# Moving pad stores, scatters, early results and sums in a fused attention and expert kernel

## The reference

```
x = x + lightning_attn(layernorm(x))   # 16 heads, chunked linear attention with decay
x = x + ffn(layernorm(x))              # 32 experts, first use
x = x + softmax_attn(layernorm(x))     # 16 heads, 4 shared key/value heads
x = x + ffn(layernorm(x))              # 32 experts, second use, the same weights

ffn(x):  probs = softmax(x @ gate_weight.T);  top_vals, top_idx = top_k(probs, 8)
         keep the first experts until their renormalised sum reaches 0.8, renormalise
         out  = sum over kept experts e of  ce[e] * (silu(g_e) * u_e) @ down_e.T
                with  g_e, u_e = split(x @ gate_up_e.T)      # 96 values each
```

## Time and profile before

| what | value |
|---|---|
| runs | 1075.89, 1076.09, 1078.5 us, median 1076.09 |
| profiled execution | 1081.71 us, span 1079.9 us |
| PE / DVE / ACT / POOL busy | 883.9 / 581.2 / 554.6 / 627.0 us of the span |
| lightning | 0 to 268 us |
| experts "f" | 269 to 509 us |
| attention | 510 to 804.5 us |
| experts "g" | 805 to 1079.9 us |

### The profile page before, as it was taken

One profiled execution on the slowest core, in us unless ns is written; L12 is line 12 of the kernel. 1 busy time (PEld: TensorE's weight loads), 2 busy tenths in 40 slices (PEclk: granted clock), 3 DMA queues, 4 the chain that ended last, 5 costly groups with the idle time before them and its releaser, 6 DMA issues. The chain is left out here.

```text
span 1079.9 us, 20627 instructions
## 1 busy us (share of the span) xinstructions
PE 883.9 (82%) x5504; PEld 670.5 (62%) x5504; DVE 581.2 (54%) x2104; ACT 554.6 (51%) x1116; POOL 627.0 (58%) x600
## 2 busy tenths in 40 slices
PE   5999899884789799998378997987758989999940
PEld 3566666553778699997243443543328879999930
DVE  4566676866572122326776488765635422222665
ACT  6333356651345365655268776775514544556520
POOL 2465537775777777775730010374754777777771
PEclk9999989986799999999679998989887999999985
DMA  9600002261768876783431011135336788777776
GB/s 338 254 1 1 1 31 87 74 242 68 244 216 304 281 241 215 221 263 122 159 137 35 35 35 41 44 123 217 128 112 205 257 293 277 235 215 251 269 252 205
DMA packets 93231, 181.64 MB, mean 168 GB/s; under 512 B 18985, under 2 KB 73788, under 8 KB 92736
## 3 DMA queue, kind: packets, MB, share of 16 engines
q1 hardware_dynamic: 68544, 114.19, 33.1%
q0 software_dynamic: 24576, 66.13, 16.7%
HBM read 96.34 MB, written 92.27 MB: 175 GB/s over the span
## 5 line engine op out<-in xcount | busy, mean ns | idle before, releaser
L1317 POOL DMA_INDIRECT result_rows<-ys,result_slots x288 | 290.8, 1010 | 87.9 <-issue 80.6
L1002 POOL DMA_INDIRECT expert_rows<-route_rows,index x224 | 223.5, 998 | 76.8 <-issue 65.1
L1968 ACT ACTIVATE b_probs<-ps 128x1024 f32<-128x1024 f32 x128 | 127.8, 1031 | 39.5 <-PE ps L1817 39.0
L1469 PE MATMUL ps<-w_gu,g_xts 128*128 x576 | 109.0, 333 | 2.3 <-issue 1.4
L1469 PE MATMUL ps<-w_gu,f_xts 128*128 x576 | 108.5, 332 | 2.6 <-ACT f_xts L1512 1.8
L1469 PEld LDWEIGHTS ps<-w_gu,g_xts 128*128 128x128 f32 x576 | 94.5, 195 | 3.8 <-issue 3.6
L1469 PEld LDWEIGHTS ps<-w_gu,f_xts 128*128 128x128 f32 x576 | 93.9, 194 | 4.2 <-issue 4.0
L1562 DVE SCALAR_TENSOR_TENSOR g_h<-ps,g_xs,g_gate 128x96 f32<-128x96 f32 x144 | 39.3, 313 | 87.8 <-ACT g_gate L1519 78.9
L1562 DVE SCALAR_TENSOR_TENSOR f_h<-ps,f_xs,f_gate 128x96 f32<-128x96 f32 x144 | 39.2, 313 | 86.7 <-ACT f_gate L1519 77.7
L1530 ACT COPY ys<-ps 128x512 f32<-128x512 f32 x144 | 83.5, 580 | 2.0 <-PE ps L1488 1.9
L1829 PE MATMUL ps<-b_probs,b_v_pad 128*32 128x512 f32 x512 | 75.2, 661 | 11.0 <-DVE b_v_pad L2101 5.5
(11 more groups left out here) (362 smaller groups left out, 1831.8 us busy)
## 6 DMA issues: line engine op xcount, KB each, us to landing
parts<-result_rows SPq DMA_DIRECT2D x32, 896.0 KB, 4.9
f_xs<-expert_rows SPq DMA_DIRECT2D x144, 160.0 KB
g_xs<-expert_rows SPq DMA_DIRECT2D x144, 160.0 KB, 2.7
expert_rows<-pad_rows SPq DMA_DIRECT2D x64, 160.0 KB
w_gu<-in_Wgu SPq DMA_DIRECT2D x1, 6144.0 KB, 18.4
expert_rows<-pad_rows SPq DMA_DIRECT2D x1, 5120.0 KB, 29.2
result_rows<-ys,result_slots POOLq DMA_INDIRECT x288, 3.3
f_w_d<-in_Wdown SPq DMA_DIRECT2D x1, 4096.0 KB, 15.4
```

Of the source, the lines that this page charges most:

```text
L1002: self.nc.gpsimd.indirect_dma_start(xs, bass.IndirectOffsetOnAxis(self.index[:, f, t, r:r + 1].bitcast(U32), 0), self.x_rows(f)[:, t, :], ...
L1317: self.nc.gpsimd.indirect_dma_start(self.y_dram, bass.IndirectOffsetOnAxis(self.slots[:, i, j:j + 1].bitcast(U32), 0), self.ys[:, i, j, :] ...
L1469: ins = nc.tensor.matmul(ps[:, bank_gu[u % 2], j * GU:(j + 1) * GU], xts[:, u % 2, o:o + P], w_gu[:, k, bass.ds(experts[j] * GU, GU)], sta ...
L1968: nc.scalar.activation(probs[:, u % RING, :, :], ps[:, 2 * (u % 2):2 * (u % 2) + 2, :], ACT.Exp, scale=float(HD) ** -0.5).then_inc(exp_don ...
```

## The change

1. Lightning's POOL issues four scatters of batch 2 at its end (`IN_DRAIN = 4`, two each in its last two units with such places), and "f" starts batch 2 at its fifth scatter.
2. The pads go out at u = 11, 13, ..., 25 in place of 17 to 24. `pads` is worked out in routing step 12 of batch 3, behind the index, with a semaphore of its own, `padded`, and SP waits for that instead of the list.
3. PE and ACT do the routing steps of slot 0 ahead of the turn and eviction of pair 0, instead of at the end of slot 0.
4. In "g" POOL scatters the results of pairs 0 and 1 (four transfers) ahead of batch 3's scatters; in "f" none.
5. The sums of "g" start at slot 59 instead of 62. A load stands three slots behind the slot of its sum: so "g" loads where it did (62, 64, ...), and "f", whose sums stay at 66, loads at 69, 71, 73, 75.

```
-                    scattered = 0
+                    scattered = 4                                   # use "f"
+            at = 2 * (unit - B * UNITS - 2 * QUADS)                 # lightning's scatters
+            if 0 <= at < IN_DRAIN:
+                yield B - 2, at
+                yield B - 2, at + 1
...
+            if f == B - 1:                                           # step 12, DVE
+                dve.wait_ge(self.counted, f + 1)
+                nc.vector.tensor_scalar(self.pads[:, :], self.count[:, 0, :], -1.0, None, ALU.add).then_inc(self.padded, 1)
...
-                    routing.wait_tiles(sp, LAST)
+                    sp.wait_ge(routing.padded, 1)
-                if PADS_AT <= u < PADS_AT + E // PADS:
-                    store_pads(PADS * (u - PADS_AT), PADS)
+                nth = (u - PADS_AT) // PADS_EVERY                    # 11, 2
+                if (u - PADS_AT) % PADS_EVERY == 0 and 0 <= nth < E // PADS:
+                    store_pads(PADS * nth, PADS)
...
+            for step, f in steps_at(0):                              # PE; ACT the same
+                routing.tensor(pe, step, f, bank_route, apart=True)
...
+        def early_pairs(scattered):
+            return 2 if (Routing.ALL - scattered) // 2 <= placed + 1 else 0
...
+            if u == left - 1:
+                for v in range(early):
+                    yield v
...
-            first, count = (62, NT) if last else (66, TT)
+            first, count = (59, NT) if last else (66, TT)
+        def loads_at(u, last):
+            return sums_at(u - 3, last)
```

More of the change, by code:

```diff
@@ L158, in lightning @@
     WITH_POWER = 3
+    IN_DRAIN = 4
     with ExitStack() as ctx:
@@ L967, in __init__ @@
         self.chosen_ready, self.pos_ready, self.index_ready = sem("chosen_ready"), sem("pos_ready"), sem("index_ready")
-        self.counted, self.listed = sem("counted"), sem("listed")
+        self.counted, self.listed, self.padded = sem("counted"), sem("listed"), sem("padded")
         self.scattered = [sem(f"scattered{f}") for f in range(B)]
@@ L1266, in list_tiles @@
             steps(nc.vector.tensor_tensor(self.row[:, :], self.row[:, :], self.valid[:, :], ALU.add))
-            if final:
-                steps(nc.vector.tensor_scalar(self.pads[:, :], self.count[:, 0, :], -1.0, None, ALU.add))
-            else:
+            if not final:
                 steps(nc.vector.tensor_scalar(flat(self.used), flat(self.since), -1.0, float(tiles), ALU.mult, ALU.add))
@@ L1352, in experts @@
     FLUSH = 4
-    PADS_AT = 17
+    PADS_AT = 11
     PADS = 4
+    PADS_EVERY = 2
+    assert PADS_AT + PADS_EVERY * (E // PADS - 1) < (TILES - PHASES[-1][1]) // 2
     LOADED = [COVERED[sum(t >= n for n in (2 * TT, 3 * TT, 3 * TT + TT // 2))] // 2 for t in range(NT)]
@@ L1502, in _ @@
                     down(u - 3, held.pop(u - 3))
-                for step, f in steps_at(u):
+                for step, f in steps_at(u) if u > 0 else ():
                     routing.tensor(pe, step, f, bank_route, apart=True)
@@ L1531, in keep_result @@
                                ps[:, bank_y[u % 2], :].rearrange("p (j n) -> p j n", j=2)).then_inc(y_ready, 1)
+            for step, f in steps_at(0):
+                routing.scalar(act, step, f, bank_route)
             for u in range(PAIRS + FLUSH):
@@ L2270, in scatters_at @@
                 yield B - 1, at + 1
+        def early_pairs(scattered):
+            return 2 if (Routing.ALL - scattered) // 2 <= placed + 1 else 0
         def results_at(u, scattered, last):
-            left = (Routing.ALL - scattered) // 2
+            left = max((Routing.ALL - scattered) // 2, placed)
             pairs = TILES // 2 if last else TILES // 2 - LATER
-            if u == max(left, placed) + Routing.ALL // 2:
-                for v in range(pairs):
+            early = early_pairs(scattered)
+            if u == left - 1:
+                for v in range(early):
+                    yield v
+            if u == left + Routing.ALL // 2:
+                for v in range(early, pairs):
                     yield v
         def sums_at(u, last):
-            first, count = (62, NT) if last else (66, TT)
+            first, count = (59, NT) if last else (66, TT)
             at = u - first
@@ L2313, in program @@
                         lambda u: scatters_at(u, scattered), lambda u: results_at(u, scattered, final),
-                        lambda u: sums_at(u, final), lambda u: sums_at(u, final), out_rows if final else None,
+                        lambda u: loads_at(u, final), lambda u: sums_at(u, final), out_rows if final else None,
                         weights_ready(use))
```

## The result

The changed kernel took 1072.55 us (median of 20 runs, 1069.7 to 1078.53) against 1080.47 for the kernel before in the same session (20 runs, 1074.99 to 1083.84): a ratio of 0.9929, with a 95% interval of 0.9914 to 0.9944, so 0.7% faster. The forecast was 1069.4 from a median of 1076.09, a ratio of 0.9938.

The account below looks back on a forecast made before the run. No engine is full throughout; PE's waits for tiles, POOL's scatters and the end chain of loads and sums bound it. 1081.71 - 1.6 ("f") - 5.1 ("g") = 1075.0, less 5.62 to the median: 1069.4 us; range 1062.5 to 1078.

Parts of the forecast that it names:

- nothing else there is late: the barrier comes 5.1 later: End of lightning: four more scatters ahead of POOL's drain, 1.28 us each, move the barrier 5.1 us later.
- rival A: Lightning's drain: the four scatters are free there and the barrier stays, giving 1064.3 us; chance 0.13.
- -1.6: Stage "f": it ends with POOL's drain, 1.6 us earlier, though PE's chain alone would give -4.2.
- The stall it began with: "f", pairs 21 to 27: PE loses 12.1 us waiting for tiles while SP issues pads.
- What was to be left of it, 2 us: "f": with pads spread, about 2 us of PE's 12.1 us wait for tiles remain.
- Its last scatter stays at 502.4 and its drain at 507.5: POOL in "f": it loses nothing, since the four scatters held before the barrier are gone behind it.
- -5.1: Stage "g": scatters decide its end, not sums; the second sum ends at 1070.7 us against 1075.84.
- The terms for POOL: "g": batch 3 starts 4.4 us later, four fewer end scatters give -5.1, folds +0.9; last result scatter +0.2.
- The term for the folds, +0.9: "g": earlier sums put about two more DVE folds beside result scatters, each stretching one by 0.47 us.
- The mis-sized term: End of "g": last scatter lands after 3.3 us, two loads together take 6.1, the second sum ends at 1070.7.
- B: Rival, both stalls: DMA engines limit transfers, not SP's order, so spreading pads relieves nothing; 1077.0 us; chance 0.15.
- C: Rival, slower: spread pads cost SP over 3.6 us a batch, deciding from 4.5; at 5.0, 1082.5 us; chance 0.12.

Follow-up runs that it names:

- the repeat: The kernel before, unchanged, run once more for a second trace: 1079.81 us, ratio 0.9998.

## Why the prediction was right, and where its steps were off

**Direction and size.** The forecast of the ratio, 0.9938, lies in the measured interval. The parts came out less evenly: "f" and "g" together gave 10.2 us in the traces where 6.7 were forecast, attention took 3.5 back that the forecast had at nothing, and lightning was 1.3 shorter by chance. The mechanism held in "g"; that the whole came so near is in part luck.

**The barrier of lightning.** The step that failed is "nothing else there is late: the barrier comes 5.1 later". It came 3.3 later: from DVE's drain, 2.9 us with no scatters (four traces), 3.6 with two, 6.2 with four (6.1 to 6.2 in six of eight traces, 7.1 in the others), 16.9 with twelve. The first 1.8 us of scatters were free, so rival A was right by a third. What held the barrier in the kernel before, 5.7 us after the start of POOL's last scatter where 3.8 and 3.9 sufficed with two and four, was not found.

**"f".** -1.6 was forecast with POOL at the end; measured were some -2.4, between -0.4 and -4.4 by which traces are paired, and POOL at the end in one trace of two (and in six of the eight other kernels with the pads spread). (The forecast's sum for PE's chain is -4.3, not -4.2; nothing hangs on it.) The stall it began with was that of one trace. In the repeat it was 7.6, and POOL ended "f" there by itself, so that no gain of PE could have counted. What was to be left of it, 2 us, was 1.5 and 5.2; over all traces it is 1.5 to 7.9 in ten with the pads spread and 6.5 to 12.1 in the four without, so the groups overlap. "Its last scatter stays at 502.4 and its drain at 507.5" failed by the scatters that were free in lightning: POOL's drain ended "f" 240.8 to 242.5 us after lightning's DVE drain in four traces with none of them, and 239.0 to 240.8 in eight with four, on the mean 241.6 and 239.9. That POOL stands close behind PE is what kept the forecast from -10, and this the rows show: in all traces but that with twelve scatters the two chains of "f" end within 4 us of each other. The kernel with the pads alone does not settle how much POOL held back, as PE lost 7.9 there.

**"g".** -5.1 was forecast, -7.8 measured. The terms for POOL were right: batch 3 started 32.8 us after the barrier instead of 28.0, +4.7 (forecast +4.4), and the last result scatter at 251.8 and 250.8 lies beside the 252.1 and 249.0 of before (forecast +0.2). The term for the folds, +0.9, is too small to be told: beyond 0.975 each, the result scatters of "g" took 4.7 and 2.2 us in the two traces before and 5.0 and 4.2 after. The mis-sized term stands behind it. The last scatter landed after 2.08 us, not the 3.3 of the median, and load and two sums took 9.8, not 10.7: the first of the two loads landed after 4.65, as a lone one does, and the second, issued 0.84 behind it, had landed when the first sum was done, 6.3 later. From the last scatter's start to the end that is 16.1 instead of 18.1. The Trainium skill, "DMA: Bandwidth & Descriptors", section "Anatomy of one DMA — SWDGE (gpsimd) path", fits a DMA of this kind with 2.0 us plus its bytes over 436 GB/s; for 131 KB that is an estimate of 2.3. The trace agrees for this last scatter with nothing behind it, at 2.08, and not for the median, 3.3.

**PE in "g"** was 5 to 6 us earlier at its last pair, not 3.5, as hardly a stall was left. What it was earlier beyond POOL did not count, since POOL ended the stage, as forecast.

**The other parts.** The order of slot 0, the early pairs and the drain were forecast at 1 us or less each, and no time shows them. The gain that the times show rests on two of five parts, the pads and the sums: without the pads the ratio is 0.9965, without the sums 0.9966, and with the pads alone 0.9949. In "g" the pads alone have 270.4 and the others without the pads 271.1, of the 275.4 before and the 267.9 and 267.2 after. That the sums come to as much as the time says is not shown: the trace gives them 1.4 us and the rest to PE, which was later there.

**The rivals.** B falls in "g": with the pads alone spread the stall is 1.0 instead of 8.6 and 7.1, while the DMA engines are as busy, 0.86 to 0.90 in the changed kernel. In "f" it is only weakened, since stalls of 4.9 to 7.9 remained in four of ten traces. C falls: a batch of pads cost 3.4 us, not 4.5.

**What the prediction left out** is attention, "moved as a whole". It is 2 to 6 us longer in ten of twelve traces with parts of the change; in the traces this is why gains of about 10 in "f" and "g" come to 8 over the whole, as they do in the medians, 7.9.

## What to carry to other kernels

Before a stall is priced, ask which other chain ends its stage and how far behind it is: here a stall of 12.1 us in "f" could be worth 1.6 at most, since POOL stood that close behind, and in "g" the sums could use 1.4 of 6.8. Work moved across a barrier is paid for on the other side, and only what fits the idle time there is free: two scatters held lightning's barrier 0.7 us and not 2.6, and four in "g" cost nothing that shows. Take a stage from two traces before a term of a few microseconds is read from one: the stall that this forecast began with was 12.1 in one trace and 7.6 in the next.

## What was not expected of the hardware

A stage that the change does not touch, attention, differs by up to 5.9 us between traces. The clock that PE is granted in it differs too, 0.74 to 0.91 in its third 20 us, but not in step with the length. SP's reads of the list took 1.26 us in the median while pads went out and 0.48 behind them. And lightning's barrier comes 3.8 to 5.7 us after the start of POOL's last scatter; the longest time is that of the kernels with none of the extra scatters in front of it, not of those with twelve (4.4).
